# A mixture-of-experts kernel: where and how far ahead its tiles' input rows are listed, gathered, cut to fp16 planes and transposed

## The reference, cut to what matters

```python
x = x + xattn(ctx, layernorm(x), Wq, Wk, gamma)   # top 153 of 512 scores kept, made symmetric
h = layernorm(x)                                  # 2048 tokens x 512
logits = h @ router_weight.T + router_bias        # 16 experts, 4 kept, softmax over the 4
gate_up = einsum('th,ehd->etd', h, gate_up_proj) + bias      # 512 -> 1024, fp32
gate, up = min(gate_up[..., ::2], 7), clip(gate_up[..., 1::2], -7, 7)
out = einsum('etd,edh->eth', (up + 1) * gate * sigmoid(1.702 * gate), down_proj) + bias
x = x + (out * score).sum(over the kept experts)
```

## Time and profile before

| | us |
|---|---|
| median of 3 runs (1051.58 to 1053.58) | 1051.64 |
| the profiled execution's own time | 1054.07 |
| its span, first to last instruction | 1052.1 |
| PE busy | 807.4 (77%) |
| DVE busy | 620.9 (59%) |
| ACT busy | 437.3 (42%) |
| POOL busy | 310.8 (30%) |

### The profile page before, as it was taken

How to read it: one execution, slowest core, us unless ns; L and a number is a source line. 1 busy time by engine, 2 the same in 40 slices (tenths; PEclk the granted TensorE clock), 3 DMA queues, 4 the chain that set the end, 5 groups by cost and what they waited for, 6 DMA issues and landing times.

```text
span 1052.1 us, 16627 instructions
## 1 busy us (share of the span) xinstructions
PE 807.4 (77%) x3294; PEld 627.6 (60%) x3295; DVE 620.9 (59%) x1137; ACT 437.3 (42%) x732; POOL 310.8 (30%) x352
## 2 busy tenths in 40 slices
PE   4474565688988977778968688788796969788984
PEld 2153355566766756657757566567575757566773
DVE  4788798765565646464636365656565564656452
ACT  4989884233433424242424243444342343333231
POOL 2224577452232311222313122213121212232222
PEclk9665655697999988898989898899998989999998
DMA  8302213547595396788686778978969587944443
GB/s 280 130 1 80 27 55 80 182 110 187 101 173 119 68 161 128 157 131 152 103 154 104 153 111 169 135 167 169 196 104 180 92 122 128 161 95 79 80 81 46
DMA packets 143581, 130.22 MB, mean 124 GB/s; under 512 B 102758, under 2 KB 105062, under 8 KB 143462
## 3 DMA queue, kind: packets, MB, share of 16 engines
q1 hardware_dynamic: 32454, 74.22, 25.1%
q0 software_dynamic: 18416, 36.53, 22.5%
q10 hardware_dynamic: 92592, 18.25, 15.6%
HBM read 84.05 MB, written 28.90 MB: 107 GB/s over the span
## 4 chain that ended last, share of the span: by engine, by line
PE 32%; DMA 23%; issue 8%; DVE 6%; ACTq 3%; ACT 3%; DVEq 2%; POOL 0%; POOLq 0%
PE bank L898 17%; DMA xg<-xn_rows,gslot 16%; PE gate_up_ps L898 14%; DMA gslot<-slot_rows 6%; DVE hl L1095 2%; DVE w L1132 2%; ACT x L646 1%; DVE xl L1085 1%; DMA out_dram<-yb,aslot 1%; PE bank L888 1%; ACTq L263 1%; ACTq L625 1%; ACT sg L668 1%; DVE x L1090 1%; DVEq L263 1%
## 5 line engine op out<-in xcount | busy, mean ns | idle before, releaser
L898 PE MATMUL gate_up_ps<-w,xh 128*128 (+1 forms) x1152 | 368.2, 401 | 0.4 <-DVE xl L1080 0.3
L898 PE MATMUL bank<-w,hh 128*128 (+1 forms) x576 | 220.7, 470 | 136.3 <-DVE hl L1095 134.2
L898 PEld LDWEIGHTS gate_up_ps<-w,xh 128*128 128x128 f32 x1152 | 215.2, 192 | 44.0 <-issue 1.0
L898 PEld LDWEIGHTS bank<-w,hh 128*128 128x128 f32 x576 | 125.6, 227 | 189.4 <-issue 160.1
L452 POOL DMA_INDIRECT out_dram<-yb,aslot x72 | 125.9, 1749 | 367.4 <-ACT yb L675 328.1
L898 PE MATMUL gate_up_ps<-w,xl 128*128 (+1 forms) x576 | 226.9, 394 | 0.0
L1090 DVE SCALAR_TENSOR_TENSOR x<-xg,x 128x512 f16<-128x512 f32 x69 | 47.7, 691 | 244.6 <-ACT x L646 244.6
L443 POOL DMA_INDIRECT xg<-xn_rows,gslot x75 | 81.0, 1080 | 256.5 <-DMA gslot<-slot_rows 158.8
L646 ACT ACTIVATE x<-xg 128x512 f16<-128x512 f32 x69 | 43.5, 631 | 227.3 <-DMA xg<-xn_rows,gslot 144.1
L898 PE MATMUL bank<-w,hl 128*128 (+1 forms) x288 | 130.0, 451 | 0.0
L898 PEld LDWEIGHTS gate_up_ps<-w,xl 128*128 128x128 f32 x576 | 109.8, 191 | 24.5
(11 more groups left out here) (213 smaller groups left out, 804.3 us busy)
## 6 DMA issues: line engine op xcount, KB each, us to landing
raw_w<-_L_ffn_gate_up_proj_dram SPq DMA_DIRECT2D x64, 512.0 KB, 4.4
raw_w<-in_L_ffn_down_proj_dram SPq DMA_DIRECT2D x64, 256.0 KB, 5.4
bgu<-n_gate_up_proj_bias_dram SPq DMA_DIRECT2D x16, 512.0 KB, 12.2
x_sb<-in_x_dram SPq DMA_DIRECT2D x4, 1024.0 KB, 11.2
xn_rows<-xn SPq DMA_DIRECT2D x4, 1024.0 KB, 6.4
out_dram<-x_sb SPq DMA_DIRECT2D x4, 1024.0 KB, 6.7
xg<-xn_rows,gslot POOLq DMA_INDIRECT x75, 4.7
out_dram<-yb,aslot POOLq DMA_INDIRECT x72, 5.0
```

Of the source, the lines that this page charges most:

```text
L898: last = nc.tensor.matmul(out_ps, lhs[:, rows], w[:, bass.ds(buf, 1), part, c, cols].rearrange("p a d -> p (a d)"), start=(m == 0), stop=( ...
```

## The change

- The slot list for the gather is loaded five tiles ahead (T+5), not three. The table word carries `slots_5` in the place of `slots_3`, so the little DVE operations that make the words have 7 columns per expert in place of 5. SP fetches the lists of tiles 4 to 8.
- The gather goes four tiles ahead (T+4), not three; `gather(4)` goes before the first addition.
- `upper_x` moves from ACT to POOL, after the gather and before `add`, and works on T+3, not T+2. `lower_x` (DVE) and `turn_x` (ACT) work on T+3 too.
- `xT16` has four buffers; they lie where `xn2` lay. One semaphore per buffer (`turned[k]`) replaces `x16_across`.
- ACT's order becomes: slot list, `high_h(T-1)`, `high_x(T+1)`, early casts, `turn_x(T+3)`, `sigmoid(T)`, `scale_y(T-1)`, late casts. DVE's becomes: `low_h(T-1)`, `low_x(T+1)`, `lower_x(T+3)`, `gate(T)`.

```diff
-          "slots_1": (0, 9, SLOTS // P), "slots_3": (9, 9, SLOTS // P)}
+          "slots_1": (0, 9, SLOTS // P), "slots_5": (9, 9, SLOTS // P)}
...
-        xT16 = sb("xT16", [P, 2, 2 * HC, P], fp16)
+        xT16 = xn2[:].rearrange("p r n -> p (r n)").bitcast(fp16).rearrange("p (k c t) -> p k c t", k=UNROLL, t=P)
...
+        turned = [sem(f"turned{k}") for k in range(UNROLL)]
...
-            for T in range(1, UNROLL):
-                k = (T + 3) % UNROLL
-                sp.wait_ge(gathered[k], 16)
-                tile = field(sp, word(sp, 1, T), "slots_3")
+            for T in range(FROZEN, FROZEN + UNROLL + 1):
+                k = T % UNROLL
+                sp.wait_ge(gathered[k], 16 * (T // UNROLL))
+                tile = field(sp, word(sp, 1, T - 1), "slots_1") if T == FROZEN else field(sp, word(sp, 1, T - 5), "slots_5")
...
+            def upper_x(T, k):
+
+                pool.wait_ge(gathered[k], slot_count(T, k))
+                if not direct(T - 2):
+                    pool.wait_ge(turned[(k - 2) % UNROLL], turn_count(T - 2, (k - 2) % UNROLL))
+                pool.sem_inc(S["turn"], 1)
+                pool.tensor_scalar(x16[:, k % 2, 0:H], xg[:, k, :], X_UNIT, None, ALU.mult).then_inc(S["x16_high"], 1)
...
             def step(T, k):
-                gather(T + 3, (k + 3) % UNROLL)
+                gather(T + 4, k)
+                upper_x(T + 3, (k + 3) % UNROLL)
                 if not known(T):
                     add(T - 1, (k - 1) % UNROLL)
...
+            gather(FROZEN, 0)
             for T in range(1, FROZEN):
-                gather(T + 3, (T + 3) % UNROLL)
+                gather(T + 4, T)
+                if not direct(T + 3):
+                    upper_x(T + 3, (T + 3) % UNROLL)
                 add(T - 1, T - 1)
...
-                if not direct(T - 2):
-                    act.wait_ge(S["xh_done"], T - 1)
-                    act.wait_ge(S["xl_done"], T - 1)
+                if known(T, DIRECT + 1):
+                    act.wait_ge(S["xn2_out"], 16 * NB)
+                if not direct(T - UNROLL):
+                    act.wait_ge(S["xh_done"], T - 3)
+                    act.wait_ge(S["xl_done"], T - 3)
                 act.sem_inc(S["turn"], 1)
-                act.dma_start_transpose(xT16[:, k % 2, :, :], x16[:, k % 2, :]).then_inc(S["x16_across"], 16)
+                act.dma_start_transpose(xT16[:, k, :, :], x16[:, k % 2, :]).then_inc(turned[k], 16)
...
-                    load_slots(field(act, offs, "slots_3"), (k + 3) % UNROLL, gslot, gslot_in)
-                if not direct(T + 2):
-                    upper_x(T + 2, (k + 2) % UNROLL)
-                if not direct(T + 1):
-                    high_x(T + 1, (k + 1) % UNROLL)
+                    load_slots(field(act, offs, "slots_5"), (k + 1) % UNROLL, gslot, gslot_in)
                 if not known(T):
                     high_h(T - 1, (k - 1) % UNROLL)
-                if direct(T + 1):
-                    high_x(T + 1, (k + 1) % UNROLL)
-                if not direct(T + 2):
-                    turn_x(T + 2, (k + 2) % UNROLL)
+                high_x(T + 1, (k + 1) % UNROLL)
                 if not known(T, FROZEN):
                     split_high(own, "early")
+                if not direct(T + 3):
+                    turn_x(T + 3, (k + 3) % UNROLL)
                 sigmoid(T, k)
...
             def step(T, k):
                 own = word(dve, 0, T)
-                if not direct(T + 2):
-                    lower_x(T + 2, (k + 2) % UNROLL)
-                if not direct(T + 1):
-                    low_x(T + 1, (k + 1) % UNROLL)
                 if not known(T):
                     low_h(T - 1, (k - 1) % UNROLL)
-                if direct(T + 1):
-                    low_x(T + 1, (k + 1) % UNROLL)
+                low_x(T + 1, (k + 1) % UNROLL)
+                if not direct(T + 3):
+                    lower_x(T + 3, (k + 3) % UNROLL)
                 gate(T, k, field(dve, own, "bias"))
```

More of the change, by code:

```diff
@@ L225, in xattn_moe_kernel @@
         posk = sb("posk", [P, RT, TOP_K])
-        near = sb("near", [P, 5])
+        near = sb("near", [P, 7])
         turns = sb("turns", [P, 2, E])
@@ L232, in xattn_moe_kernel @@
         spare = hotv[:].rearrange("p r k e -> p (r k e)")
-        past, held = (spare[:, i * 5 * E:(i + 1) * 5 * E].rearrange("p (t e) -> p t e", e=E) for i in range(2))
-        which, block_at = sb("which", [P, 5]), sb("block_at", [P, 5])
+        past, held = (spare[:, i * 7 * E:(i + 1) * 7 * E].rearrange("p (t e) -> p t e", e=E) for i in range(2))
+        which, block_at = sb("which", [P, 7]), sb("block_at", [P, 7])
         move, flag = sb("move", [P, 4]), sb("flag", [P, 8])
@@ L276, in direct, with turn_count @@
             return known(T, DIRECT)
+        def turn_count(T, k):
+            done = slot_count(T, k) - 16
+            return done if k else done - 16
         def slot_count(T, k):
@@ L382, in _ @@
             pool.iota(pad_i, pattern=[[1, (SLOTS + P) // P]], base=0, channel_multiplier=1).then_inc(c, 1)
-            pool.iota(near[:], pattern=[[1, 5]], base=-1, channel_multiplier=1, **kw).then_inc(c, 1)
+            pool.iota(near[:], pattern=[[1, 7]], base=-1, channel_multiplier=1, **kw).then_inc(c, 1)
             pool.memset(fill[:], float(P - 1)).then_inc(c, 1)
@@ L478, in _ @@
             pool.sem_inc(S["all_added"], 1)
-            for k in range(3):
+            for k in range(UNROLL):
                 pool.wait_ge(gathered[k], 16 * final + 32)
             pool.wait_ge(aslot_in[0], 16 * final + 32)
-            pool.wait_ge(S["x16_across"], 64 * final + 16 * across_dma(UNROLL + 1))
+            pool.wait_ge(gslot_in[0], 16 * final + 48)
+            pool.wait_ge(turned[0], 16 * final)
+            pool.wait_ge(turned[1], 16 * final + 16)
+            pool.wait_ge(turned[2], 16 * final + 16)
+            pool.wait_ge(turned[3], 16 * final)
             pool.sem_inc(S["turn"], 1)
@@ L921, in step @@
                 pe.wait_ge(S["lo_done"], need)
+                if not direct(T):
+                    pe.wait_ge(S["xh_done"], T + 1)
                 pe.wait_ge(S["xl_done"], T + 1)
@@ L1293, in _ @@
             send(V.tensor_scalar(total_i[:], cum[:, E - 1:E], -1.0, None, ALU.add))
-            link(V.tensor_tensor(past, near[:].unsqueeze(2).broadcast_to([P, 5, E]),
-                                 cum[:].unsqueeze(1).broadcast_to([P, 5, E]), ALU.is_ge))
+            link(V.tensor_tensor(past, near[:].unsqueeze(2).broadcast_to([P, 7, E]),
+                                 cum[:].unsqueeze(1).broadcast_to([P, 7, E]), ALU.is_ge))
             low_x(1, 1)
@@ L1299, in _ @@
             send(V.tensor_reduce(which[:], past, AX.X, ALU.add))
-            link(V.tensor_tensor(held, past, room[:].unsqueeze(1).broadcast_to([P, 5, E]), ALU.mult))
+            link(V.tensor_tensor(held, past, room[:].unsqueeze(1).broadcast_to([P, 7, E]), ALU.mult))
             send(V.tensor_reduce(block_at[:], held, AX.X, ALU.add))
```

17 lines of the change are left out of this document (6 added, 11 removed).

## The result

| | before | after | predicted |
|---|---|---|---|
| median, us | 1051.66 | 938.10 (934.3 to 940.31) | 983 |
| ratio, with its 95% interval | 1 | 0.8912 (0.8877 to 0.8948) | 0.935 |
| profiled execution's own time / span, us | 1054.07 / 1052.1 | 934.3 / 932.4 | 983.6 (span) |
| down product of tile 3 to that of tile 70, us | 773.35 | 651.1 | 701 |
| period of the 39 plain / 28 split tiles, mean us | 10.75 / 12.65 | 9.01 / 10.71 | 8.9 / 11.4 |

The account below looks back on a forecast made before the run. Late gathers and slot lists, passed on by ACT's in-order queue, were taken to hold PE. Tiles: 39 × 8.9 + 319 + 35 = 701 against 773.35 us, 72 saved, less 3.5: 68.5, so 983 us; 8-in-10 range 925 to 1030.

Parts of the forecast that it names:

- The bound before: Late gathers and slot lists hold ACT's in-order queue and then PE; 121 of 773 us hang on them.
- Plain tiles: The 39 tiles without a weight split: 8.9 us each between down products, with 1.5 us of slack.
- Price of `upper_x` on POOL: The multiplication moved to POOL: 0.8 us, between 0.61 and 2.30, covered by slack in plain tiles, so cost 0.
- Split tiles: The 28 tiles with weight splits, in 14 pairs: 10.9 us for the first, 11.9 for the second, 319 us together.
- The residual for late gathers: Gathers beside a weight load still exceed the lead: 2.5 us per expert, 35 us in all, ends 0 and 75.
- The start: At tiles 2 and 3, `lower_x(5)` stands ahead of `gate(2)` on DVE: 3.5 us lost, bounds 0 and 7.
- signs of being wrong: `upper_x` over 2 us on average, plain tiles over 9.5 us, or DVE's `lower_x` waits over 100 us that PE repeats.
- B: Rival: lead grows over plain tiles, hiding even 14 us gathers, and split tiles don't grow; 934 us, chance 0.23.
- C: Rival: transfers stay late, DMA share rising to 0.84 in a shorter stretch; 1020 us, chance 0.20.
- D: Rival: POOL's `upper_x` and DVE block each other; slower from a mean `upper_x` of 3.0 us; 1085 us, chance 0.06.

Follow-up runs that it names:

- b: Changed kernel with `upper_x(T+3)` back on ACT, behind `high_x`: 886.48 us, ratio 0.847 to the kernel before; repeated at 0.843.
- c: Changed kernel with POOL's `upper_x` made longer by writing a second block of 512 columns that nobody reads: 1016.59 us, ratio 0.970 to the kernel before.
- e: Kernel before with only the transpose `turn_x(T+2)` moved behind the early casts: 1029.86 us, ratio 0.987.
- f: Changed kernel with the transpose back beside the gather, `turn_x(T+2)` right behind `high_x(T+1)`: 952.47 us, ratio 0.911 to the kernel before.
- l: Kernel before with one more wait ahead of the transpose, for `low_h(T-1)` on DVE: 996.09 us, ratio 0.948.
- i: Kernel before with only the new orders on ACT and DVE, plus one more wait on PE: 962.29 us, ratio 0.922.
- g: Changed kernel with `upper_x(T+3)` ahead of the gather on POOL: 920.32 us, ratio 0.881 to the kernel before.
- run a: Changed kernel with `lower_x` behind `gate` on DVE and `turn_x` behind `scale_y` on ACT: 1039.67 us, ratio 0.996 to the kernel before.

## Why the prediction was right in direction and 45 us off

All times here are of the profiled execution: 119.7 us of span gained. The earlier trace rows give what was known before.

- *The bound before.* Right: late gathers and lists, repeated by ACT's queue, hold PE. PE's wait fell to 48.7 us (about 60 forecast), the clock rose to 0.98, the list wait to 4.1 us.
- *Plain tiles.* Forecast 39 × 8.9 = 347, measured 39 × 9.01 = 351.4. The length is right, the reason isn't: not PE's 8.9 but POOL's loop of 9.00 sets it; with the loop gone (b) the usual step from `gate` to `gate` is 8.65. Without `upper_x` the loop is 7.5 us, so against b's 8.65 there was room for 1.15 us of it, where the forecast had counted on 1.5.
- *Price of `upper_x` on POOL.* Taken at 0.8 us, measured 1.69 in the mean: the term was mis-sized by a factor of two, though inside its bounds of 0.61 and 2.30. I chose the cast of the same columns as the nearest row; the cast of before took 0.61 us for 80 × 512 into fp32r, and a scaling into fp16 took 1.49 at its least. With 0.8 there would have been slack left; with 1.5 there was none, and c shows that each 0.1 us of it is then worth some 6 us.

  The Trainium skill's figure of 769 ns (GPSIMD Engine Reference, Elementwise — side-by-side cycle accounting), its best case for 512 elements, is half of what these 70 operations took at their least. The Trainium skill, SBUF — State Buffer, Who interferes with whom, says that a DVE instruction with two SBUF inputs contends with a GpSimd instruction that reads SBUF. The rows agree: 19 of the 70 ran beside DVE's weight subtractions and took 2.07 to 2.19 us, as the second of the two in the rows below.

```profile
425.75 1.53 POOL L458 TENSOR_SCALAR x<-xg 128x512 f16<-128x512 f32 x1
...
435.06 2.12 POOL L458 TENSOR_SCALAR x<-xg 128x512 f16<-128x512 f32 x1
```

- *Split tiles.* Forecast 14 × (10.9 + 11.9) = 319, measured 28 × 10.71 = 299.9. In most pairs the second is longer than the first, as forecast (10.4 and 11.2; 10.1 and 10.9), but the first is shorter than 10.9, which was read from one tile of before, where the mean was 12.65. In b they are 9.4 to 9.5: most of what I took for the price of splitting goes with `upper_x` on POOL. One term was wrong by its mechanism: the transpose's issue waits for `lower_x` and not for the casts (e), so the casts don't push it, and the sigmoid behind it, back by the 0.9 us that were forecast.
- *The residual for late gathers.* This is the step that failed: "35 us per 14 experts, since those beside a weight load take 12.7 to 14.5". Measured 0: none took over 8.2. The landing time was taken as a property of a gather beside a weight load. The runs showed that it hangs on the transpose that leaves beside it (f brings lateness back, l takes it away with one wait), and the change moves just that. Had it stayed, the lead would have left about 20 us of it at most (f): the 35 were of the right order for that case.
- *The start.* +1.1 us from tile 1 to 3, against +3.5. Before tile 1 −3.2, which I had not foreseen, behind tile 70 +4.7 (21.2 to 25.9), neither priced.

Together: +4.4 (plain) −19 (split) −35 (gathers) −2.4 (start) +1.5 (the two ends) is −50.5 against the forecast span of 983.6, and the measured span is 932.4, 51.2 under it; the rest is rounding.

Of the signs of being wrong one was touched: DVE's `lower_x` kept 103.0 us of waits, but PE waited only 48.7 before the down product. The other two stayed away (1.69 us against 2, 9.01 against 9.5).

Of the rivals, B's time was hit while its condition (the lead grows until 14 us fit) wasn't tested by the change: no gather took 14 us. C was opposite to what happened: the DMA share fell. D had the right place, POOL and `lower_x` ahead of `gate`, and the right mechanism; its price of 3.0 us wasn't reached. In c the mean was 2.96, and that kernel still gained 3.0%: D's threshold was too low, since it was worked out from a gain of 68.5 us and not of 113.6. B's number is in part luck, then: its 8.9 and 10.9 fit, but there was no late gather left to hide.

Where the gain comes from: lists alone 2.4%, the wait that moves the transpose 5.2%, the new orders 7.8%, all of the change 10.9%, all of it with `upper_x` left on ACT 15.3 to 15.7%. The parts overlap and don't add up, as each also makes gathers less often late.

What stays open is the exact condition. In the kernel before, late gathers always had both neighbours close, the load within about 2.5 us and the transpose mostly within 1 us, and without a load within several us none took over 5.8. But no single rule fits all runs. The distance between transpose and gather doesn't decide alone: in l four gathers (395.49, 579.58, 658.16, 692.33) had the transpose only 0.3 to 0.4 us behind them and a load begun 1.1 us ahead, and landed in 7.1 to 7.8 us. Nor does the order of transpose and load: in the kernel before the transpose left ahead of the load's last piece, the biases, in every slow case that had one, and in i and l behind it, but in g it left 1.0 us behind it and five recorded gathers still took 10.5 to 12.2 us.

## What to carry to other kernels

Before you build a lead that hides a slow transfer, look at what else leaves in the microsecond of the slow ones and not of the fast ones: a single wait that moved one of them by a microsecond gave half of what the whole restructuring did (5.2 of 10.9%). When work moves onto an engine that is half idle, follow the order of every queue once round from a tile's instruction to the same one of the next tile; if the moved work lies on that loop and the loop is the longest, its length counts in full in each tile, and idleness of the engine says nothing (POOL was busy for 47%). Cutting such a loop only helps if the next one round another queue is shorter (run a).

## What the hardware did that I had not expected

- Gather, 2-plane DMA transpose and weight load within 1.2 us: at 365.59 the gather took 14.5 us, the transpose 15.0 and the bias load 14.2, while the two large weight pieces landed in 5.8 and 7.0. With the transpose at 1.57 us (355.03 in i) the gather took 6.2, the bias load 6.8, the weight pieces 5.0 and 5.9. In f transposes took up to 16.4 us.
- A DMA issue on ACT's queue isn't held by ACT's running casts, only by a wait ahead of it (e: issued at 359.10 within casts of 358.62 to 361.47).
- POOL's scaling of 128 × 512 fp32 to fp16 took 1.49 us at its least (1024 columns 2.77), ACT's 0.62. Even POOL's gather issue, undisturbed 1.00 us, was stretched to 2.41 beside DVE's weight subtractions:

```profile
423.27 2.41 POOL L449 DMA_INDIRECT xg<-xn_rows,gslot  x1 [0.30 <-issue]
```
